# Two 257-key attentions: minima that also copy the masked scores, a new order of steps, and semaphores cleared inside the next stage

## The reference, cut to what matters

```python
scores = einsum(q_heads, k_heads)            # 16 heads x 32 queries x 257 keys
scores = where(mask, NEG, scores)            # l2x only, one mask row for all batches
p = softmax(scores)                          # over the 257 keys
x = x + (p @ v_heads).merge() @ Wo + bo
```

## Time and profile before

| | |
|---|---|
| Time before, median of 3 executions | 3632.56 us (3627.05 to 3634.94) |
| The profiled execution: its time, its span | 3634.64 us, 3632.9 us |
| TensorE busy | 2984.3 us, 82% |
| VectorE busy | 2467.4 us, 68% |
| ScalarE busy | 2004.9 us, 55% |
| GpSimd busy | 1886.7 us, 52% |
| Maxima of `l1x_att`, first and last start | 727.1 and 1147.9 us |
| Maxima of `l2x_att`, first and last start | 1685.0 and 2141.5 us |

### The profile page before, as it was taken

The page is one execution under the profiler, slowest core; times in us unless marked ns, Lnnn a source line. Parts: engine busy times, 40 slices in busy tenths (PEclk is TensorE's granted clock), DMA queues, the critical chain, the costliest instruction groups (busy, mean ns, idle before and its releaser), DMA issues. The chain is left out here.

```text
span 3632.9 us, 79346 instructions
## 1 busy us (share of the span) xinstructions
PE 2984.3 (82%) x23799; PEld 2036.6 (56%) x23799; DVE 2467.4 (68%) x6665; ACT 2004.9 (55%) x6297; POOL 1886.7 (52%) x2012
## 2 busy tenths in 40 slices
PE   6989698889998998686999987878772768869967
PEld 5769534466665875454777762333341436736645
DVE  7876677778887671536888876989876123457863
ACT  5545405688887554135777765555530125559954
POOL 5640203677776880263666647888840531117730
PEclk9999889999999999798999998989885888978989
DMA  3210002422221000211111114434430229900000
GB/s 106 88 33 0 6 1 80 120 79 80 79 81 54 1 7 0 75 54 41 36 36 38 36 32 145 141 134 141 140 140 4 34 40 244 203 8 2 2 7 23
DMA packets 142432, 233.68 MB, mean 64 GB/s; under 512 B 28796, under 2 KB 104862, under 8 KB 141575
## 3 DMA queue, kind: packets, MB, share of 16 engines
q1 hardware_dynamic: 134088, 221.61, 20.8%
q0 software_dynamic: 8128, 9.45, 1.4%
HBM read 200.44 MB, written 13.71 MB: 59 GB/s over the span
## 5 line engine op out<-in xcount | busy, mean ns | idle before, releaser
L3238 PE MATMUL l2a_pY<-l2a_hc,ident 128*128 128x512 f32 x512 | 275.2, 677 | 89.9 <-POOL l2a_hc L3157 55.3
L2476 POOL TENSOR_TENSOR l2x_att_prob<-l2x_att_prob,l2x_att_rs 128x1024 f32<-128x1024 f32 x128 | 242.4, 1894 | 144.8 <-DVE l2x_att_rs L2707 144.8
L3127 POOL TENSOR_TENSOR l2a_dbu<-l2a_dx,l2a_BC 128x1024 f32<-128x1024 f32 x128 | 298.5, 2353 | 21.3 <-PE l2a_pY L3238 10.7
L2476 POOL TENSOR_TENSOR l1x_att_prob<-l1x_att_prob,l1x_att_rs 128x1024 f32<-128x1024 f32 x128 | 242.4, 1894 | 107.1 <-DVE l1x_att_rs L2707 107.1
L2664 ACT ACTIVATE l2x_att_prob<-l2x_att_pS,l2x_att_nmx 128x257 f32<-128x257 f32 x512 | 236.3, 475 | 92.1 <-DVE l2x_att_nmx L2702 92.1
L3255 ACT ACTIVATE l2a_pA<-l2a_dl,l2a_A 128x512 f32<-128x512 f32 x256 | 174.4, 689 | 188.0 <-DVE l2a_pH L3361 112.2
L2664 ACT ACTIVATE l1x_att_prob<-l1x_att_pS,l1x_att_nmx 128x257 f32<-128x257 f32 x512 | 236.3, 474 | 73.0 <-DVE l1x_att_nmx L2702 72.9
L3238 PEld LDWEIGHTS l2a_pY<-l2a_hc,ident 128*128 128x128 f32 x512 | 103.8, 211 | 253.0 <-issue 120.3
L2702 DVE TENSOR_REDUCE l1x_att_nmx<-l1x_att_pS 128x1 f32<-128x257 f32 x512 | 182.0, 418 | 88.3 <-PE l1x_att_pS L2575 88.3
L3361 DVE TENSOR_TENSOR_SCAN l2a_pH<-l2a_pA,l2a_dbu 128x512 f32<-128x512 f32 x192 | 224.8, 1216 | 23.3 <-POOL l2a_dbu L3127 11.8
L2702 DVE TENSOR_REDUCE l2x_att_nmx<-l2x_att_pS 128x1 f32<-128x257 f32 x512 | 182.0, 418 | 49.9 <-PE l2x_att_pS L2580 49.9
(11 more groups left out here) (766 smaller groups left out, 8940.7 us busy)
## 6 DMA issues: line engine op xcount, KB each, us to landing
l2a_BC<-l2a_rows SPq DMA_DIRECT2D x128, 512.0 KB, 3.7
l3x_att_ctn<-ctx_n SPq DMA_DIRECT2D x32, 576.0 KB, 14.5
l0x_att_kvs<-ctx_t SPq DMA_DIRECT2D x32, 514.0 KB, 3.5
l1x_k_xin<-ctx_t SPq DMA_DIRECT2D x32, 514.0 KB, 3.5
l1x_att_ctx<-ctx_t SPq DMA_DIRECT2D x128, 128.5 KB, 2.1
l1x_att_kT<-l1x_KA SPq DMA_DIRECT2D x128, 128.5 KB, 2.2
l2x_att_ctx<-ctx_t SPq DMA_DIRECT2D x128, 128.5 KB, 2.1
l3x_att_ctx<-ctx_t SPq DMA_DIRECT2D x32, 514.0 KB, 12.6
```

The lines of the kernel that those rows point to most:

```text
L2476: pool.tensor_tensor(p, p, bc(rs[:, b, :], 2, LAST), ALU.mult).then_inc(scaled, 1)
L3127: pool.tensor_tensor(dbu[:, u % 3], dx[:, g % 2], bc(BC[:, u % RING, 0, :], 1, NC), ALU.mult).then_inc(dbu_made, 1)
L3238: last = pe.matmul(pY[c][:, :], env.ident[:, :], hc[:, u % 3, c, :], start=False, stop=n == NS - 1)
```

## The change

Four things change in the attentions, and one in all stages.

1. The maximum becomes a minimum of negated, masked scores, taken by one instruction that also copies: `tensor_tensor_reduce` reads a bank of `pS` and the mask row, writes minus their sum to `prob` in SBUF and its minimum to `nmx`. In `l1x`, which has no mask, the mask row is zero. The exponentials read `prob` in place, with scale -1. The mask matmuls, `sel_b`, `mask_b` and `selq` go away.
2. `scores` of a unit waits for the minima of the unit before it, no longer for its exponentials.
3. The keys of `l2x` are made in the first bank of `pS`, after the first minimum of the unit that is there, instead of in `pKV`; so the values no longer wait for the copy of the keys, and `scores` alone waits for it.
4. The order within a slot is new. TensorE: scores, transposes (second bank first), attend, tails or output, keys, last keys, values. VectorE: the copy of the keys comes after `own_head`, tails and output. ScalarE: the turned probabilities are kept ahead of the exponentials. GpSimd: queries, bias and last values ahead of `scale`. VectorE's slots are all unrolled; those of the other engines stay in the loop.
5. The clearing blocks go. A stage's semaphores stay allocated until GpSimd, at the start of the next stage that opens, has raised that stage's semaphores and then cleared those that ended; one block at the end of the program clears the rest.

```diff
@@ stage
+        def open_(pool):
+            for s in primed + [opened]:
+                pool.sem_inc(s, 1)
+            while ENDED:
+                cleared.append(ENDED.pop())
+                clear(pool, cleared[-1][0])
...
-        with nc.Block() as block:
-            @block.gpsimd
-            def _(pool):
-                for low, high in zip(starts, ends):
-                    pool.sem_clear(range(low, high))
+        ENDED.append(([s.num for s in sems], held))
+        for _, free in cleared:
+            free.close()
+def clear(pool, numbers):
+    starts = sorted(k for k in numbers if k - 1 not in numbers)
+    ends = sorted(k + 1 for k in numbers if k + 1 not in numbers)
+    for low, high in zip(starts, ends):
+        pool.sem_clear(range(low, high))
@@ cross_attention, GpSimd
                 def slot(n, c, k):
-                    if inside(n):
-                        scale(n, c)
-                        if c >= 2:
-                            tails(c, k)
                     if inside(n + 2):
                         queries(n + 2, c + 2)
...
+                    if inside(n):
+                        scale(n, c)
+                        if c >= 2:
+                            tails(c, k)
@@ TensorE
                 def keys(n, c, k):
                     pe.wait_ge(landed[c % 2], landed_count(c, k, 2))
-                    bank_read(n, c, k)
-                    pe.matmul(pKV[:, 0:KEYS], wk[:, :], ctx[:, c % 2, 0:KEYS]).then_inc(k_made, 1)
+                    after(pe, m_made, R * (n - 1))
+                    pe.matmul(pS[:, 0, 0:KEYS], wk[:, :], ctx[:, c % 2, 0:KEYS]).then_inc(k_made, 1)
 
                 def bank_free(n, c, k):
-                    if KA is None:
-                        pe.wait_ge(k_kept, made(n))
-                    else:
-                        pe.wait_ge(landed[c % 2], landed_count(c, k, 2))
-                        bank_read(n, c, k)
+                    pe.wait_ge(landed[c % 2], landed_count(c, k, 2))
+                    after(pe, v_kept, n - 1)
+                    if c == 1:
+                        after(pe, mo_kept, k - 1)
...
-                    after(pe, p_made, n - 1)
+                    after(pe, m_made, R * (n - 1) + R - 1)
                     for j in range(R):
                         r = slice(32 * j, 32 * j + 32)
-                        last = pe.matmul(pS[:, j, 0:KEYS], qb[r, b].rearrange("p h q -> p (h q)"), kT[r, b, 0:KEYS],
-                                         start=True, stop=not masked)
-                    if masked:
-                        for j in range(R):
-                            r = slice(32 * j, 32 * j + 32)
-                            last = pe.matmul(pS[:, j, 0:KEYS], sel_b[r].rearrange("p h q -> p (h q)"), mask_b[r, :],
-                                             start=False, stop=True)
+                        last = pe.matmul(pS[:, j, 0:KEYS], qb[r, b].rearrange("p h q -> p (h q)"), kT[r, b, 0:KEYS])
                     last.then_inc(s_made, 1)
...
                     if inside(n + 1):
                         scores(n + 1, c, k)
+                    if inside(n - 1):
+                        turn(n - 1, (c - 1) % 4, 1)
+                        turn(n - 1, (c - 1) % 4, 0)
...
                         keys(n + 2, c, k)
-                    if inside(n - 1):
-                        turn(n - 1, (c - 1) % 4, 0)
-                        turn(n - 1, (c - 1) % 4, 1)
@@ ScalarE
-                        last = act.activation(prob[:, b, j, 0:KEYS], pS[:, j, 0:KEYS], ACT.Exp,
-                                              bias=nmx[:, b, j:j + 1], accum_out=sums[:, b, j:j + 1])
+                        last = act.activation(prob[:, b, j, 0:KEYS], prob[:, b, j, 0:KEYS], ACT.Exp,
+                                              bias=nmx[:, b, j:j + 1], scale=-1.0, accum_out=sums[:, b, j:j + 1])
...
                 def slot(n, c, k):
-                    if inside(n + 1):
-                        exponentials(n + 1, (c + 1) % 4, k if c < 3 else k + 1)
                     if inside(n - 1):
                         keep_turned(n - 1, (c - 1) % 4)
+                    if inside(n + 1):
+                        exponentials(n + 1, (c + 1) % 4)
@@ VectorE
-                def maxima(n, b):
+                def maxima(n, b, k):
+                    after(dve, t_made, 2 * (n - 4) + 1)
+                    after(dve, tail_kept, 2 * (k - 1) + (b == 3))
                     dve.wait_ge(s_made, made(n))
                     for j in range(R):
-                        dve.tensor_reduce(nmx[:, b, j:j + 1], pS[:, j, 0:KEYS], AX.X, ALU.max, negate=True
-                                          ).then_inc(m_made, 1)
+                        dve.tensor_tensor_reduce(prob[:, b, j, 0:KEYS], pS[:, j, 0:KEYS], mask[:, :], -1.0, BIG,
+                                                 ALU.add, ALU.min, nmx[:, b, j:j + 1]).then_inc(m_made, 1)
...
-                run_slots4(dve, slot, B, -2, 3)
+                for n in range(-2, B + 3):
+                    slot(n, n % 4, n // 4)
```

More of the change, by code:

```diff
@@ L81, in stage @@
             pair=lambda name: [loop_sem(f"{name}_a"), loop_sem(f"{name}_b")],
-            open=lambda pool: [pool.sem_inc(s, 1) for s in primed + [opened]],
+            open=open_,
             opened=opened,
         )
-        numbers = sorted(s.num for s in sems)
-        starts = [k for k in numbers if k - 1 not in numbers]
-        ends = [k + 1 for k in numbers if k + 1 not in numbers]
-        with nc.Block() as block:
-            @block.gpsimd
-            def _(pool):
-                for low, high in zip(starts, ends):
-                    pool.sem_clear(range(low, high))
+        ENDED.append(([s.num for s in sems], held))
+        for _, free in cleared:
+            free.close()
+ENDED = []
+def clear(pool, numbers):
[3 more added lines that the diff above has]
+        pool.sem_clear(range(low, high))
 def bc(ap, axis, n):
@@ L2424, in cross_attention @@
             loads += [(wk[:, :], w.wk), (cols[:, 0:1], w.bk), (cols[:, 1:2], w.bv)]
+        mask = st.sb("mask", [P, KEYS])
         if masked:
[L2426 to L2429 removed]
+            mask_i = st.sb("mask_i", [P, KEYS], I32)
+            loads += [(mask_i[:, :], w.mask)]
         pS = st.ps("pS", [P, R, 512])
@@ L2595, in attend @@
                 def attend(n, b, k):
+                    pe.wait_ge(t_kept_a, made(n))
                     pe.wait_ge(t_kept_d, made(n))
-                    pe.wait_ge(t_kept_a, made(n))
                     pe.wait_ge(v_kept, made(n))
@@ L2657, in last_keys, with exponentials @@
                     act.activation(mt[:, :], M, ACT.Copy).then_inc(mo_kept, 1)
-                def exponentials(n, b, k):
-                    after(act, t_made, 2 * (n - 4) + 1)
-                    after(act, tail_kept, 2 * (k - 1) + (b == 3))
+                def exponentials(n, b):
                     for j in range(R):
                         act.wait_ge(m_made, made(R * n + j))
-                        last = act.activation(prob[:, b, j, 0:KEYS], pS[:, j, 0:KEYS], ACT.Exp,
-                                              bias=nmx[:, b, j:j + 1], accum_out=sums[:, b, j:j + 1])
+                        last = act.activation(prob[:, b, j, 0:KEYS], prob[:, b, j, 0:KEYS], ACT.Exp,
+                                              bias=nmx[:, b, j:j + 1], scale=-1.0, accum_out=sums[:, b, j:j + 1])
                     last.then_inc(p_made, 1)
                 def keep_turned(n, b):
-                    act.wait_ge(t_made, made(2 * n + 1))
+                    act.wait_ge(t_made, made(2 * n))
                     after(act, o_made, n - 2)
@@ L2711, in keys @@
                     after(dve, s_made, n - 2)
-                    dve.tensor_scalar(kT[:, c % 2, 0:KEYS], pKV[:, 0:KEYS], cols[:, 0:1], None, ALU.add
+                    dve.tensor_scalar(kT[:, c % 2, 0:KEYS], pS[:, 0, 0:KEYS], cols[:, 0:1], None, ALU.add
                                       ).then_inc(k_kept, 1)
@@ L2726, in keep_turned @@
                 def keep_turned(n, b):
-                    dve.wait_ge(t_made, made(2 * n))
+                    dve.wait_ge(t_made, made(2 * n + 1))
                     after(dve, o_made, n - 2)
@@ L2753, in slot @@
                     if inside(n + 1):
-                        maxima(n + 1, (c + 1) % 4)
-                    if inside(n + 2) and KA is None:
-                        keys(n + 2, c)
+                        maxima(n + 1, (c + 1) % 4, k if c < 3 else k + 1)
                     if inside(n - 2):
@@ L2762, in slot @@
                         add(k - 1)
+                    if inside(n + 2) and KA is None:
+                        keys(n + 2, c)
                     if inside(n - 1):
@@ L3970, in build, with _ @@
             layer(nc, env, a)
+    with nc.Block() as block:
+        @block.gpsimd
+        def _(pool):
+            for numbers, _ in ENDED:
+                clear(pool, numbers)
+    while ENDED:
+        ENDED.pop()[1].close()
```

31 lines of the change are left out of this document (13 added, 18 removed).

## The result

The changed kernel takes 3617.68 us (median of 9, 3604.80 to 3620.77) against 3632.56 us beside it. The ratio is 0.9949, with a 95% interval of 0.9934 to 0.9964: faster by 0.5%, 13 to 24 us by the interval. Foretold were 3566 us and at most 3603, so the sign was right and about three quarters of the gain is missing. The profiled execution took 3614.32 us, with a span of 3612.5 us. All ratios leave out executions in a slower state of the chip; there is one, of `e1_blocks`, at 3756.17 us.

The account below looks back on a forecast made before the run. It took a loop through three engines to bound `l1x`, full TensorE `l2x`, and clearing blocks the time between stages. Gains of 24 (blocks), 36 (`l1x`) and 8 (`l2x`), 68 from 3634.6, gave 3566 us; range 3545 to 3603.

Parts of the forecast that it names:

- the loop of `l2x`: In `l2x`, scores through attend, key product and copy back to scores: 3.35 us a plain slot, period 3.53, 8 us gained.
- Transposes to attend: Term of the key loop in `l2x`: time from the start of the transposes to attend, put at 0.83 us.
- The hand-over from the copy to TensorE: Last term of the key loop in `l2x`: from the end of the keys' copy to TensorE's next start, 0.07 us.
- Tails, output and last keys: In `l2x`, extra work in three of four slots, adding 0.17 us to the plain slot in the mean, as before.
- TensorE's wait for `kT`: In plain slots of `l2x`, TensorE was to wait about 0.1 us for the copied keys.
- The copy of the keys costs more: Rival, chance 0.14: in `l2x` 0.15 us more than before per unit, costing 19 us instead of giving 8; 3593 us.
- `l1x`: mechanism: In `l1x`, the loop through three engines goes and TensorE becomes full: period 3.31 to 3.03 us, 36 us gained.
- PE decides with 3.00: In `l1x`, TensorE's work of 3.00 us per unit sets the pace, before ACT with 2.91 and DVE with 2.85.
- The minimum: VectorE's new instruction in both attentions: 0.37 us between two starts, 0.334 to 0.40 likely, against 0.334 for the old maximum.
- The half rate: Rival, chance 0.04: the minimum starts every 0.60 us and VectorE bounds both attentions, 142 us lost against 24; 3752 us.
- The exponentials: On ScalarE, reading SBUF instead of PSUM: 0.04 us more each, 0.16 per unit, 2.91 in `l1x` and 2.96 in `l2x`.
- The blocks: Between stages, removing the clearing blocks takes 26 us off and GpSimd's clears cost 2: gain 24 us (19 to 26).

Follow-up runs that it names:

- e1_blocks: The kernel before with only the clearing blocks gone (new `open_` and `clear`), both attentions as before: 3622.72 us, 0.9946 of the kernel before.
- e3_key_wait_last: The changed kernel with `scores` waiting for the copy of the keys last instead of second: 3602.61 us, 0.9917 of the kernel before.
- e6_half_copy: The changed kernel with VectorE copying only 129 of the 257 key columns in `l2x`, a timing test: 3599.69 us, 0.9897 of the kernel before.
- e4_keys_before_attend: The changed kernel with the key product of `l2x` ahead of attend and its copy ahead of `own_head`: 3582.33 us, 0.985 of the kernel before.
- e5_l1x_order: The changed kernel with the old order in `l1x`: transposes behind attend, ScalarE's copy behind the exponentials: 3636.09 us, 0.9993 of the kernel before.
- e9_l1x_split_exps: The changed kernel, in `l1x` with TensorE's old order and ScalarE's copy between second and third exponential: 3629.51 us, 0.9987 of the kernel before.
- e2_l1x_new_l2x_before: The changed kernel with the attention of the kernel before for `l2x` alone: 3591.64 us, 0.9875 of the kernel before.
- e7_fewer_waits: The changed kernel without four TensorE waits that an earlier wait already covers: 3617.99 us, 0.994 of the kernel before.

## Why the prediction was wrong, step by step

- **The step that failed: the loop of `l2x`.** "So the plain slot falls from 3.42 to 3.35 only" measured 3.72, and the period 3.90 instead of 3.53. The loop, its members and their order were right; two of its terms were too small.
  - *Transposes to attend*, 0.83 from the earlier trace rows, was a step to values of the same tile shape; to attend it is 1.03.
  - *The hand-over from the copy to TensorE* was put at 0.07, from 1908.97 to 1909.04 in the earlier trace rows. With another wait behind it, as in the new `scores`, it is 0.24; `e3_key_wait_last` takes 0.12 of that off. The row showed no hand-over at all: in this slot, as in 26 of 39 from 1800 to 2000 us, the values start 0.98 behind the transposes, when the loads of those end (1908.06 + 1.01 = 1909.07), and the copy had ended by then. In the other 13 they start 1.08 behind and 0.05 behind the copy, so 0.07 was near the truth by luck, for a wait that stands last. Why 0.12 and not 0.05 are left in `e3_key_wait_last` is open.
  - *Tails, output and last keys* add 0.17 to the plain slot in the mean, as foretold, but by luck: output adds 0.52 where it added 0.31 before, tails add 0.18 where they added 0.06, and last keys add nothing.
  - TensorE's wait for `kT`, foretold as 0.1 in a plain slot, is 0.33. `e6_half_copy` shows that the loop sets the period, and `e4_keys_before_attend`, which takes attend, tails and output out of it, brings the 3.59 of before back.
- **The rival that came true was too small.** "The copy of the keys costs more" charged 0.15 over before; it was 0.30. I priced it as some lost cover, not as a loop with each hand-over at its dearest, and so the range ended at 3603. With 0.24 for the last hand-over alone, the plain slot would have come to 3.52, above the 3.42 of before.
- **`l1x`: mechanism right, size off.** TensorE is full and its wait gone, as foretold. The period is 3.11 instead of 3.03, 25 us won instead of 36. The term is "PE decides with 3.00": it was counted with the old order, and the new one has one change of shape more, 0.19 (0.83 to 1.02). The rise is only 0.11, since 3.00, the busy time of the earlier trace rows, was more than the groups needed: at their own distances they come to 0.65 + 0.57 + 0.83 + 0.65 = 2.70 in a plain slot, as `e5_l1x_order` then measured (2.69), and now to 2.88. Tails, output and last keys add 0.22 in the mean. `e5_l1x_order` and `e9_l1x_split_exps` show what the extra change buys: without it ScalarE's copy is waited for and the unit takes 3.22.
- **The minimum: right.** In the timeline four start at 1901.30, 1901.65, 1902.00 and 1902.35: x = 0.35 (0.37 taken). The accumulator read of 83 ns lies under the next one. The half rate of the Trainium skill's Vector Engine (DVE) Microarchitecture Reference (section Points that are easy to get wrong) does not come in, as its letter said: one source is PSUM, and 0.60 would have been needed.
- **The exponentials: right.** They are 499 ns long instead of 475, and start every 0.49 us (905.80, 906.29) instead of every 0.45 (903.76, 904.21 before): 0.04 more, as charged. The work per unit in `l1x` is 2.88 us of ScalarE and 2.79 of VectorE, where 2.91 and 2.85 were foretold.
- **The blocks: right within the scatter.** 20 and 30 us by two pairs, 28 by the profiles, 24 foretold. (The 0.07 charged for each block is the same 0.07 of the earlier trace rows that was no hand-over.) One block is left, and its clears stand in GpSimd's queue:

```profile
L105 POOLq EVENT_SEMAPHORE_RANGE_CLEAR  x146: 44/45/224, 26.8 to 3612.0; - x146
```

Open: what makes the stretch behind `l2x` scatter by 20 us, which is what blurs the worth of the blocks; why the scores of `e2_l1x_new_l2x_before` wait longer for the exponentials than those of before; and why `l2x` took 3.64 in `e1_blocks`. For this last, the first 50 us of that stage had a granted clock of 0.87 instead of 0.99 and 527 matmuls instead of 574, which would be most of the 6 us, an estimate. That the marked gaps belong to changes of tile shape is argued from their places, from `e7_fewer_waits` and from the plain slots of `e5_l1x_order`; no run changed a shape alone.

## What to carry to other kernels

When a product and its copy move behind other work, write out the whole loop through them, take each hand-over from a row with the same things behind it, and move the product so early that a full group of matmuls lies beside the copy: here one move of `keys` and its copy shortened `l2x` by 39 us, and the kernel by 36 by the ratios. Put the wait that comes last at the end of its list. And count the changes of weight tile shape in a TensorE slot as work, here 0.19 us each, but do not pay for one less with a hand-over. A busy time read from a window is no floor: the distances between the starts of the groups are.

## What the runs showed of the hardware

- TensorE's weight loads run ahead of the matmuls of a group of the same tile shape (1908.06 against 1908.44), and stand still at a change of shape: 0.33 us from 32\*128 to 128\*128 or 128\*32, 0.17 from 128\*128 to 128\*32 behind transposes and 0.33 behind the key product, 0.20 from 128\*32 to 128\*128 or 32\*32. The matmuls stay busy in these gaps; one change more cost 0.19 us a slot (2.69 against 2.88). Leaving out three waits ahead of attend did not shorten its gap (`e7_fewer_waits`).
- A wait of TensorE that was satisfied already cost 0.12 us when it followed the late one (0.24 against 0.12 in 52 slots each); waits left out under running matmuls gave nothing back (`e7_fewer_waits`).
- The combined add, minimum and copy of 257 fp32 columns from PSUM and SBUF to SBUF starts every 0.35 us on VectorE, 0.02 above the plain maximum that it replaces.
